# Routing by sequences: the sums over 64 tokens as two-column products on TensorE

## The reference

```
x = x + tanh(g_xattn[0]) * cross_attention(layernorm(x), ctx, ctx)
x = x + tanh(g_ffn[0])   * two_layers(layernorm(x))
x = x + tanh(g_xattn[1]) * gated_attention(layernorm(x), ctx, ctx)
x = x + tanh(g_ffn[1])   * int8_product(layernorm(x))

# inside two_layers, for layer l:
    x = x + attn(ln(x, ln1_w[l], ln1_b[l]))
    h = ln(x, ln2_w[l], ln2_b[l])          # (x - mean) / sqrt(var + eps) * w + b
    x = x + (token_moe if l == 0 else seq_moe)(h)

def seq_moe(h, gw, gb, w1, b1, w2, b2):    # h: 64 x 64 x 128
    cw = combine_weights(h.mean(axis=1) @ gw + gb)   # best two of 8 experts a sequence
    ...                                     # each sequence goes through its two experts
```

## Time and profile before

| | us |
|---|---|
| median of 3 runs | 1057.99 |
| lowest and highest run | 1056.52, 1062.42 |
| profiled execution, its own time | 1067.39 |
| its span, first to last instruction | 1065.7 |
| TensorE, matmuls busy | 893.0 (84%) |
| TensorE, weight loads busy | 720.7 (68%) |
| VectorE busy | 711.9 (67%) |
| ScalarE busy | 695.2 (65%) |
| GpSimd busy | 514.6 (48%) |

### The profile page before, as it was taken

The page is one execution under the profiler, slowest core; times in us unless marked ns, Lnnn a source line. Parts: engine busy times, 40 slices in busy tenths (PEclk is TensorE's granted clock), DMA queues, the critical chain, the costliest instruction groups (busy, mean ns, idle before and its releaser), DMA issues.

```text
span 1065.7 us, 34734 instructions
## 1 busy us (share of the span) xinstructions
PE 893.0 (84%) x11689; PEld 720.7 (68%) x11693; DVE 711.9 (67%) x1935; ACT 695.2 (65%) x1940; POOL 514.6 (48%) x893
## 2 busy tenths in 40 slices
PE   4999999999974799999289999975899998869904
PEld 3788877888853499999166666763677776837601
DVE  5878888888868666666367777858321212857796
ACT  3888878999945577777257767844455554338754
POOL 7333334666660355553678888510433332028716
PEclk9999999999976899999669999977999999979955
DMA  4100050000002122222111000520000000611002
GB/s 109 55 17 16 16 165 2 4 0 0 1 2 79 26 66 67 64 64 60 40 27 26 20 25 26 182 62 1 1 0 0 0 0 21 138 45 36 20 1 79
DMA packets 53202, 41.64 MB, mean 39 GB/s; under 512 B 11176, under 2 KB 45716, under 8 KB 53124
## 3 DMA queue, kind: packets, MB, share of 16 engines
q1 hardware_dynamic: 48220, 31.50, 10.7%
q0 software_dynamic: 4320, 8.86, 3.4%
q10 hardware_dynamic: 584, 0.26, 0.1%
HBM read 27.42 MB, written 9.24 MB: 34 GB/s over the span
## 4 chain that ended last, share of the span: by engine, by line
PE 62%; DVE 12%; issue 8%; POOLq 7%; POOL 6%; ACT 2%; DMA 1%; DVEq 1%; SPq 0%; ACTq 0%
PE ps_st L1220 17%; PE ps_o L1220 16%; PE ps_v L1322 10%; PE ps_xa L1220 9%; PE ps_v L1220 5%; POOLq L841 5%; PE ps_o L1344 3%; POOL work L842 2%; POOLq L831 1%; PE ps_xa L1264 1%; DVE y L1745 1%; DVE work L1911 1%; DVE probs_t L1915 1%; DVE recip L1742 1%; DVE work L1866 1%
## 5 line engine op out<-in xcount | busy, mean ns | idle before, releaser
L758 POOL TENSOR_TENSOR shared<-kts,kmask 128x256 f32<-128x256 f32 x192 | 135.8, 729 | 165.1 <-ACT qts L944 89.5
L1220 PE MATMUL ps_st<-work 128*128 128x128 f32 (+1 forms) x872 | 153.1, 319 | 19.7 <-POOL work L842 12.6
L1220 PEld LDWEIGHTS ps_st<-work 128*128 128x128 f32 x872 | 123.6, 191 | 43.5 <-POOL work L842 26.6
L975 ACT COPY probs_t<-ps_v 128x512 f32<-128x512 f32 x192 | 112.4, 586 | 49.4 <-PE ps_v L1322 47.8
L1723 DVE TENSOR_REDUCE rowmax<-ps_st 128x16 f32<-128x1024 f32 x96 | 117.5, 1224 | 26.2 <-PE ps_st L1220 22.0
L1322 PE MATMUL ps_v<-ident,work 128*128 128x128 f32 x768 | 125.6, 288 | 3.1 <-ACT probs_t L975 2.1
L1731 DVE TENSOR_TENSOR work<-ps_st,rowmax 128x1024 f32<-128x1024 f32 x96 | 116.6, 1215 | 0.0
L800 POOL DMA_INDIRECT xg<-x_rows,row_from x71 | 76.3, 1075 | 80.4 <-PE ps_xa L1406 59.2
L967 ACT ACTIVATE work<-work 128x512 f32<-128x512 f32 x192 | 110.4, 622 | 5.2 <-DVE work L1731 2.3
L1220 PE MATMUL ps_o<-shared,probs_t 128*64 128x18 f32 x3072 | 109.1, 212 | 2.0 <-issue 1.0
L1113 ACT ACTIVATE probs_t<-ps_st,b1s 128x256 f32<-128x256 f32 x152 | 59.5, 475 | 73.8 <-PE ps_st L1220 73.8
(11 more groups left out here) (380 smaller groups left out, 2108.9 us busy)
## 6 DMA issues: line engine op xcount, KB each, us to landing
y_rows<-work SPq DMA_DIRECT2D x71, 64.0 KB
w<-in_L_ffn_e_w_dram SPq DMA_DIRECT2D x2, 2048.0 KB, 10.9
w<-rhs_const SPq DMA_DIRECT2D x2, 1536.0 KB, 11.1
x_res<-in_x_dram SPq DMA_DIRECT2D x4, 512.0 KB, 6.6
ctx_in<-in_ctx_dram SPq DMA_DIRECT2D x32, 64.0 KB, 1.8
x_rows<-h_all SPq DMA_DIRECT2D x1, 2048.0 KB, 8.7
ctx_dup<-in_ctx_dram SPq DMA_DIRECT2D x32, 64.0 KB, 1.8
out_dram<-x_res SPq DMA_DIRECT2D x16, 128.0 KB, 1.8
```

The source lines that it names most:

```text
L758: i = pool.tensor_tensor(km[:, par, g, :, :], kts[:, par, g:g + 1, :].to_broadcast([P, KM_HEADS, SEQ]), kmask[:, :, :], ALU.mult)
L975: nc.scalar.copy(probs_t[:, par, 512 * half:512 * half + 512], ps_v[:, :]).then_inc(S["pts_ready"], 1)
L1220: return nc.tensor.matmul(o, a, b, start=start, stop=stop, skip_group_check=True)
```

## The change

The sums over the tokens move from VectorE to TensorE. A constant `halves` (128x2: ones for the tokens of the first sequence in column 0, for those of the second in column 1) is multiplied with each normed tile as it is: the result is 128 channels by 2 sequences, in PSUM (`row_sums`, 32 products into 64 columns of `ps_t`). Weight and bias are applied to the sums, in one operation of VectorE (64 * bias is made ahead of it). All eight groups of normed tiles have their own place in `work` (`xw8`), so `seq_norm` waits for nothing. The transposes and affines stay, since the experts need `h_t`, but those of groups 5 to 7 go behind the routing product. ScalarE's exponential goes ahead of its last affine. The small products of the routing have other columns of PSUM (`ps_t` in place of `ps_a`), and TensorE waits for all affines (`pre_sb`) ahead of the transpose of `cw`.

The diff, whole:

```diff
--- before.py
+++ after.py
@@ -265,6 +265,8 @@
 
         before = sb("before", [NSEQ, NSEQ])
         ones_seq = sb("ones_seq", [NSEQ, P])
+        halves = sb("halves", [P, SPT])
+        bias_sum = sb("bias_sum", [P, 1])
         place_no = sb("place_no", [NSEQ, PLACES])
         pair_no = sb("pair_no", [1, NQUAD, NE])
         col_off = sb("col_off", [NSEQ, PLACES])
@@ -303,7 +305,6 @@
         apart = work[:, 2048:2048 + 2 * ACT_COLS * NTURN].rearrange("p (b j n) -> p b j n", b=2, n=NTURN)
         tw1s = work[:, 0:2 * DFF].rearrange("p (b n) -> p b n", b=2)
         tw2s = work[:, 2 * DFF:6 * DFF].rearrange("p (b n) -> p b n", b=4)
-        xw = work[:, 0:2 * BLK].rearrange("p (b n) -> p b n", b=2)
         xw8 = work[:, :].rearrange("p (b n) -> p b n", b=NB)
         ctx_rows = h_t
         km16 = shared[:, K_END - 2 * 4 * P:K_END].rearrange("p (b s h k) -> p b s h k", b=2, s=SPT, h=4)
@@ -738,6 +739,9 @@
                 fresh(pool.memset(before[:, :], 1.0))
                 select(before[:, :], [[1, NSEQ]], -1, -1)
                 fresh(pool.memset(ones_seq[:, :], 1.0))
+                fresh(pool.memset(halves[:, :], 0.0))
+                for half in range(SPT):
+                    fresh(pool.memset(halves[half * SEQ:(half + 1) * SEQ, half:half + 1], 1.0))
                 fresh(pool.iota(place_no[:, :], pattern=[[1, PLACES]], base=0, channel_multiplier=0,
                                 allow_small_or_imprecise_dtypes=True))
                 fresh(pool.iota(pair_no[:, :, :], pattern=[[1, NQUAD], [0, NE]], base=0, channel_multiplier=0,
@@ -1089,10 +1093,11 @@
             context_copy(1)
             row_root(CH_PRE1)
             for g in range(NB):
+                if g == NB - 1:
+                    route_exp(1, NSEQ, 1)
                 seq_affine(g)
                 if g + 2 < NB:
                     context_copy(g + 2)
-            route_exp(1, NSEQ, 1)
             nc.scalar.preload_act_table_set("gelu_and_others")
 
             def first_weights(t, par):
@@ -1372,7 +1377,7 @@
                 pe.wait_ge(S["xn_ready"], PRE1 + (g + 1) * SUB)
                 seen(pe, S["pre_sb"], NB + g - 1)
                 for q in range(SUB):
-                    i = nc.tensor.transpose((ps_x, ps_a)[g % 2][:, q * P:(q + 1) * P], xw[:, g % 2, q * P:(q + 1) * P],
+                    i = nc.tensor.transpose((ps_x, ps_a)[g % 2][:, q * P:(q + 1) * P], xw8[:, g, q * P:(q + 1) * P],
                                             ident[:, :])
                 i.then_inc(S["pre_tr"], 1)
 
@@ -1470,18 +1475,34 @@
             pe.wait_ge(S["x_updated"], UPD[1] + NT)
             context_group(1)
             context_group(2)
-            for g in range(NB):
+
+            def row_sums(g):
+
+                pe.wait_ge(S["xn_ready"], PRE1 + (g + 1) * SUB)
+                for q in range(SUB):
+                    t = g * SUB + q
+                    i = mm(ps_t[:, SPT * t:SPT * (t + 1)], xw8[:, g, q * P:(q + 1) * P], halves[:, :])
+                if g == NB - 1:
+                    i.then_inc(S["seqlog_ready"], 1)
+
+            row_sums(0)
+            for g in range(5):
                 seq_transpose(g)
                 if g + 3 < NB:
                     context_group(g + 3)
-
-            pe.wait_ge(S["hmean_ready"], NB)
-            mm(ps_a[0:NSEQ, 0:NE], hmean[:, :], gatew[:, 1, :]).then_inc(S["seqlog_ready"], 1)
+                row_sums(g + 1)
+            row_sums(6)
+            row_sums(7)
+            pe.wait_ge(S["hmean_ready"], 2)
+            mm(ps_t[0:NSEQ, 512:512 + NE], hmean[:, :], gatew[:, 1, :]).then_inc(S["seqlog_ready"], 1)
+            for g in range(5, NB):
+                seq_transpose(g)
 
             pe.wait_ge(S["route_link"], ROUTE_COUNTS)
-            mm(ps_a[0:NSEQ, 0:NE], before[:, :], counts[:, :])
-            mm(ps_a[:, NE:2 * NE], ones_seq[:, :], counts[:, :]).then_inc(S["place_ps"], 1)
-
+            mm(ps_t[0:NSEQ, 528:528 + NE], before[:, :], counts[:, :])
+            mm(ps_t[:, 528 + NE:528 + 2 * NE], ones_seq[:, :], counts[:, :]).then_inc(S["place_ps"], 1)
+
+            pe.wait_ge(S["pre_sb"], 2 * NB)
             pe.wait_ge(S["route_link"], ROUTE_LINKS)
             nc.tensor.transpose(ps_o[0:NE, 0:NSEQ], cw[0:NSEQ, 0, :], ident[0:NSEQ, 0:NSEQ]
                                 ).then_inc(S["place_ps"], 1)
@@ -1859,19 +1880,10 @@
 
             def seq_norm(g):
 
-                if g >= 2:
-                    dve.wait_ge(S["pre_tr"], NB + g - 1)
                 for q in range(SUB):
                     t = g * SUB + q
-                    V.tensor_scalar(xw[:, g % 2, q * P:(q + 1) * P], tile(inner, t), mean[:, t:t + 1], rstd[:, t:t + 1],
+                    V.tensor_scalar(xw8[:, g, q * P:(q + 1) * P], tile(inner, t), mean[:, t:t + 1], rstd[:, t:t + 1],
                                     ALU.subtract, ALU.mult).then_inc(S["xn_ready"], 1)
-
-            def seq_sum(g):
-
-                dve.wait_ge(S["pre_sb"], NB + g + 1)
-                n_ = BLK // SEQ
-                V.tensor_reduce(hmean[:, g * n_:(g + 1) * n_], h_t[:, g * BLK:(g + 1) * BLK].rearrange(
-                    "p (q i) -> p q i", i=SEQ), AXX, ALU.add).then_inc(S["hmean_ready"], 1)
 
             def find_slots():
 
@@ -2022,14 +2034,17 @@
             dve.wait_ge(S["x_updated"], UPD[1] + NT)
             dve.wait_ge(S["pool_const"], CONSTS[3])
             row_stats(CH_PRE1, 4 * NT)
-            for g in range(NB + 2):
-                if g < NB:
-                    seq_norm(g)
-                if g >= 2:
-                    seq_sum(g - 2)
-
+            for g in range(NB):
+                seq_norm(g)
+            V.tensor_scalar(bias_sum[:, :], vec_t[:, 2 * 3 + 1:2 * 3 + 2], float(SEQ), None, ALU.mult
+                            ).then_inc(S["hmean_ready"], 1)
+            dve.wait_ge(S["hmean_ready"], 1)
             dve.wait_ge(S["seqlog_ready"], 1)
-            V.scalar_tensor_tensor(logits[0:NSEQ, 0, :], ps_a[0:NSEQ, 0:NE], 1.0 / SEQ,
+            V.tensor_scalar(hmean[:, :], ps_t[:, 0:NSEQ], vec_t[:, 2 * 2 + 1:2 * 2 + 2], bias_sum[:, 0:1], ALU.mult, ALU.add
+                            ).then_inc(S["hmean_ready"], 1)
+
+            dve.wait_ge(S["seqlog_ready"], 2)
+            V.scalar_tensor_tensor(logits[0:NSEQ, 0, :], ps_t[0:NSEQ, 512:512 + NE], 1.0 / SEQ,
                                    rowb[0:NSEQ, R_GB1:R_GB1 + NE], ALU.mult, ALU.add).then_inc(S["logits_sb"], 1)
             dve.wait_ge(S["logits_sb"], 1)
             best_two()
@@ -2046,7 +2061,7 @@
                 dve.wait_ge(S["place_ps"], 2)
                 link(V.tensor_copy(cw_t[:, :], ps_o[0:NE, 0:NSEQ]))
 
-                link(V.tensor_scalar(tiles_of[:, :], ps_a[:, NE:2 * NE], 1.0 / QUAD, 0.5 - 0.5 / QUAD,
+                link(V.tensor_scalar(tiles_of[:, :], ps_t[:, 528 + NE:528 + 2 * NE], 1.0 / QUAD, 0.5 - 0.5 / QUAD,
                                      ALU.mult, ALU.add))
                 link(V.tensor_scalar(tiles_of[:, :], tiles_of[:, :], MAGIC, None, ALU.add))
                 link(V.tensor_scalar(upto_a[:, NE:2 * NE], tiles_of[:, :], MAGIC, None, ALU.subtract))
@@ -2055,7 +2070,7 @@
                     link(V.tensor_tensor(dst[:, NE:2 * NE], src[:, NE:2 * NE], src[:, NE - d:2 * NE - d], ALU.add))
 
                 link(V.scalar_tensor_tensor(place_base[:, :], upto_b[0:NSEQ, NE - 1:2 * NE - 1], float(QUAD),
-                                            ps_a[0:NSEQ, 0:NE], ALU.mult, ALU.add))
+                                            ps_t[0:NSEQ, 528:528 + NE], ALU.mult, ALU.add))
                 link(V.tensor_tensor(chosen_place[:, :, :], chosen[:, :, :],
                                      place_base[:, :].unsqueeze(1).to_broadcast([NSEQ, 2, NE]), ALU.mult))
                 link(V.tensor_reduce(place[:, :], chosen_place[:, :, :], AXX, ALU.add))
```

## The result

| | before | after |
|---|---|---|
| median of 6 runs each, us | 1058.77 | 1069.18 |
| lowest and highest run, us | 1055.92, 1062.42 | 1063.48, 1071.65 |
| ratio of times, with its 95% interval | | 1.0069 (1.0039 to 1.0099) |
| profiled execution, its own time, us | 1067.39 | 1064.26 |
| first norm to the logits, us (profile) | 13.98 | 22.20 |

The change made the kernel slower: by its ratio 7.3 us of 1058.8, with an interval of 4.1 to 10.5; the two medians lie 10.4 us apart, at the upper end of that interval. The forecast was 1057.5 with a range from 1054.6 to 1062.5. What happened is rival 1, in the largest form that the prediction priced: in the profiles the stage is 8.2 us longer up to the logits, and 8.4 us up to the first addition.

A forecast was written before the change was run, and what follows sets the result against it. Waits on VectorE's norms and sums bound the stretch before the routing product; with the new TensorE queue and VectorE operation it would start at 730.48 instead of 730.96, so 1057.99 - 0.5 = 1057.5 us, range 1054.6 to 1062.5.

The forecast's parts named there:

- rival 1: TensorE's clock falls to half while the row sums run: +2.5, +5.0 or +10.1 us (1060.0, 1062.5, 1067.6); chance 0.3.
- Norms without a break: On VectorE, 32 norms run unbroken once the sums are gone, 8.4 us, ending at 725.8.
- A pass at full clock: On TensorE, each row-sum pass costs 0.11 us, set by its 128-column weight load; 64 passes take 7.04 us.
- Rival 3: Thin row-sum passes on TensorE are cheap, 0.038 to 0.055 us: -4.3 us, 1053.7; chance 0.07.
- The new operation of VectorE: Weight and bias on 128x64 from PSUM, between sums and routing product: 0.21 us, bounds 0.16 to 0.32.
- Behind the product: Transposes, affines and a context copy moved behind the routing product: ScalarE free at 2.9 to 3.3 us, cost 0 to 0.1.
- The granted clock: TensorE's clock was taken as full for the whole queue ahead of the routing product, 11.44 us plus 0.16.
- the thin 18-column products: Trace row for rival 1: TensorE at full clock in 704 to 706 with transposes and these, at half from 707.
- Its price: Half clock on TensorE: 0.215 us a pass, 0.105 more; 96 passes from the second piece on cost +10.1 us.
- Rival 2: TensorE's clock comes back behind the routing product; table passes save up to 1.2 us, 1.4 with small products: 1056.1; chance 0.1.
- The Trainium skill's rule: Transposes don't count as busy, so TensorE's whole queue runs at half clock, +10.9 us; the prediction held it not to apply.

The follow-up runs named there:

- before_again: The kernel before with nothing changed, run and profiled a second time; ratio to the kernel before 1.0001.
- sums_first_98: The changed kernel with 98-column row sums, and only these and three context groups ahead of the routing product, the norms' transposes behind it; ratio to the kernel before 0.9966.
- sums_98_columns: The changed kernel with the row sums' constant widened from 2 to 98 columns by 96 of zeros; ratio to the kernel before 0.9992.
- change_again: The changed kernel unaltered, run once more; ratio to the kernel before 1.0074.
- sums_64_columns: The changed kernel with the row sums' constant widened from 2 to 64 columns by 62 of zeros; ratio to the kernel before 0.9988.
- sums_first_98_longer_stream: `sums_first_98` with 20 instead of 14 products that nobody reads behind the tables; ratio to the kernel before 0.9974.

## Why the prediction was wrong, step by step

- **Norms without a break**: right, 8.30 us (forecast 8.4).
- **A pass at full clock is 0.11 us, whatever its columns**: right. The whole queue took 11.63 us at full clock (forecast 11.60) with 98 columns, and the first eight passes, up to the transposes behind them, took 0.92 us with 2 columns (710.92 to 711.84) and 0.97 with 98. Rival 3 is refuted.
- **The new operation of VectorE**: 0.34 us, not 0.21, and over the upper bound of 0.32. The row it was taken from is a copy; none of the rows has an operation from PSUM with two scalars a partition. What makes it dearer isn't shown. With the clock held the logits come 0.35 us sooner than before (13.63 against 13.98), where 0.48 was forecast; this term makes up the difference.
- **Behind the product**: right in the main. The exponential starts 3.28 us behind it (forecast 2.9 to 3.3). VectorE takes the result 3.58 us behind it, 0.11 later than before. From the logits to `place_w` it is 10.92 us against 10.72, so 0.2 us was lost where 0 to 0.1 was forecast.
- **The granted clock**: this step failed. The sum took every one of its 104 passes at the full clock, 11.6 us; the queue took 20.10, with the clock at 0.50 from the second piece of row sums on. The prediction had rival 1 with the right mechanism and named the row that would show it, but put it at 0.3 and "mostly for its small forms", on this: "from 727 to 730 the clock stayed with only 1.31 us busy of 3.00". That reads busy time as what holds the clock. The runs show otherwise: half clock at 4.00 of 4.00 us busy in the change, and a clock of 1.00 at 2.46 of 4.00 and 0.94 at 1.43 of 4.00 in `before_again`, where TensorE had little but transposes. The same prediction had a row that spoke the right way, the thin 18-column products after which the clock was half, and it was weighed too lightly.
- **Its price**: nearly right. A round of 16 passes takes 3.31 us at half clock, 0.207 a pass (forecast 0.215), so 0.097 more than at full. The queue was 20.10 - 11.63 = 8.47 us longer, which at 0.097 is 87 passes; the rival had 96 at 0.105, 10.1 us. Its 96 leave out only the first eight of the 104, but the eight transposes ahead of the second piece ran at full clock too, and 88 are left.
- **Rival 2** (the clock comes back after the product) didn't show: it was 0.50 to 742 at least. In `sums_first_98` the full clock took 1.09 us off the eight table passes (1.30 against 2.39), where up to 1.2 was forecast.
- **The Trainium skill's rule** ("TensorE: Matmul & The Clock Gate", Part 4: transposes don't count as busy for the gate) would have forecast +10.9 us, nearer to the result than the forecast. The trace doesn't agree with its reason: `sums_98_columns` has the same transposes at the full clock, and so has `before_again`. What changed the clock in these runs was the width of the row sums, with the transposes as they were.

The Trainium skill, "TensorE: Matmul & The Clock Gate", Part 1 ("HAM oscillation"), puts a fall of the clock down to gaps between bursts of products. That doesn't account for the loss here: TensorE does idle 1.41 us ahead of the first row sums, but 1.42 us in `sums_98_columns` too, where the clock held, and in the change it stayed at 0.50 through 18 us without a gap.

## What to carry to other kernels

When work moves to TensorE, price it at both clocks and ask of the new instructions which clock stood in the rows where their like ran; "the engine is busy" is no answer. Thin float32 products cost as much as wide ones here (the weight load of 128 columns sets the pass), so zeros beside the wanted columns were free and kept the full clock: one line turned 1.0069 into 0.9992. The same holds within one batch: `change_again` 1.0074, `sums_64_columns` 0.9988. The gain itself came only once little but what the product needs stood ahead of it, and had then to be defended one stage on: products that nobody reads, counted so as to span a wait, end sooner when they run at the full clock, and must be counted again.

## What the runs showed that was not expected

- A stage that held the clock on transposes alone lost it when two-column products were added (1.00 to 0.50 between 701 and 705), with TensorE busier than before. In all three profiles in which sums of 2 or 32 columns began at the full clock it fell about 2 us behind the first of them and didn't come back in the stage. Of the six with 98 columns or none that were at 1.00 there, five kept it to the last sums; in `sums_first_98_longer_stream` it fell about 2 us behind the first sum too, and came back. So what is shown is that with the thin products the clock stays down, and with the wide ones it comes back or holds; that the thin ones start the fall is not shown. Why thin work does worse than idle time is open; no run had thin products without any transposes from a full clock.
- Zeros count: the 96 columns that kept the clock at 1.00 were zeros.
- The clock at the start of the stage is a matter of the execution: 1.00 at the first row sums of the change, 0.50 in `change_again`, the same kernel. A median over several runs takes it in, a single profile doesn't.
